# Latent attention and routed FFN layer on eight cores: the key-path evacuation changes engine and the routing of four tiles is batched

## What is computed

```python
x = x + _layernorm(attn(_layernorm(x)))
x = x + _layernorm(ffn(_layernorm(x)))

# attn: latent projections, 32 heads, head dim 128 + 64 rotary
q_c = rmsnorm(h @ w_qa, g_qa)            # 4096 -> 1536
kv  = h @ w_kva                          # 4096 -> 512 + 64
k_c, k_rope = kv[..., :512], kv[..., 512:]
k_c = rmsnorm(k_c, g_kva)                # then w_kvb -> keys, values
# ffn
probs = softmax(xf @ W_router.T)         # 8 experts
topk_p, topk_i = top_k(probs, 2); topk_p /= sum(topk_p)
combine = sum(one_hot(topk_i, 8) * topk_p[..., None], 1)
h = einsum('nd,erd->ner', xf, A_stack) * combine[..., None]
out = xf @ W_base.T + b_base + einsum('ner,eor->no', h, B_stack) * 2.0
```

## Time and profile before

| | |
|---|---|
| times of three runs | 4605.1, 4820.23, 4815.49 us, median 4815.49 us |
| the profiled execution | 4605.1 us |
| its span on the slowest core (core 5) | 4603.5 us |
| spans of the eight cores | 4563.3 to 4603.5 us |
| TensorE busy | 3413.5 us, 74% of the span |
| ScalarE busy | 1351.0 us, 29% |
| VectorE busy | 893.3 us, 19% |

### The profile page before, as it was taken

One profiled execution on the slowest core, in us unless ns is written; L12 is line 12 of the kernel. 1 busy time (PEld: TensorE's weight loads), 2 busy tenths in 40 slices (PEclk: granted clock), 3 DMA queues, 4 the chain that ended last, 5 costly groups with the idle time before them and its releaser, 6 DMA issues. The chain is left out here.

```text
span 4603.5 us, 43117 instructions; the slowest of 8 cores (4563.3 to 4603.5 us)
## 1 busy us (share of the span) xinstructions
PE 3413.5 (74%) x16282; PEld 1345.7 (29%) x16282; DVE 893.3 (19%) x2270; ACT 1351.0 (29%) x2038; POOL 66.6 (1%) x129
## 2 busy tenths in 40 slices
PE   2665683888888898888988889869999048834883
PEld 1333441232232322322222222224444023312331
DVE  3553014111111101111011110100000330023002
ACT  1333001344444444444444434420000230013001
POOL 0000000000000000000000000000000000000000
PEclk9777896898898888988888889879999569966996
DMA  5221411000000000000000000023332326541663
GB/s 132 89 92 45 75 28 30 16 16 3 13 16 15 16 16 1 16 15 16 15 0 16 15 16 1 0 55 73 74 64 46 136 48 110 110 114 33 110 111 109
DMA packets 31370, 218.96 MB, mean 48 GB/s; under 512 B 3888, under 2 KB 4160, under 8 KB 14784
## 3 DMA queue, kind: packets, MB, share of 16 engines
q0 software_dynamic: 17776, 147.97, 17.8%
q1 hardware_dynamic: 13392, 68.24, 4.3%
HBM read 347.37 MB, written 16.78 MB: 79 GB/s over the span
## 5 line engine op out<-in xcount | busy, mean ns | idle before, releaser
L69 ACT ACTIVATE pool<-sPP,pool 128x512 bf16<-128x512 f32 x1024 | 700.2, 687 | 588.7 <-PE sPP L69 588.3
L69 PE MATMUL sPP<-pool 128*128 128x512 bf16 (+1 forms) x2048 | 801.2, 426 | 1.7 <-DVE pool L69 1.7
L69 PE MATMUL PEp<-pool 128*128 128x128 bf16 (+2 forms) x3872 | 534.4, 290 | 171.5 <-DVE pool L69 93.7
L69 PE MATMUL PDq<-pool 128*1 128x512 bf16 (+3 forms) x1792 | 499.0, 338 | 170.7 <-DVE pool L69 125.8
L69 PE MATMUL fP<-pool 128*128 128x512 bf16 (+1 forms) x2176 | 522.6, 398 | 75.3 <-DMA pool<-wbt 37.9
L69 PE MATMUL oP<-pool 128*128 128x512 bf16 x2048 | 457.8, 388 | 57.0 <-ACT pool L69 31.1
L69 DVE BATCH_NORM_STATS2 pool<-pool 128x6 f32<-128x512 bf16 (+1 forms) x344 | 209.6, 679 | 1352.2 <-ACT pool L69 1223.9
L69 PE MATMUL PCq<-pool 128*128 128x512 bf16 x1024 | 430.9, 421 | 0.0
L69 PEld LDWEIGHTS PEp<-pool 128*128 128x128 bf16 (+1 forms) x3872 | 286.3, 97 | 413.0 <-issue 229.1
L69 ACT ACT_TABLE_LOAD x77 | 98.8, 1283 | 882.3 <-PE sPP L69 277.2
L69 DVE COPY pool<-PDq 1x1024 f32<-1x1024 f32 x64 | 78.0, 1218 | 1429.8 <-PEq L1249 1395.2
(11 more groups left out here) (58 smaller groups left out, 1067.3 us busy)
## 6 DMA issues: line engine op xcount, KB each, us to landing
pool<-wbt POOLq DMA_DIRECT2D x64, 1024.0 KB, 8.7
pool<-xb SPq DMA_DIRECT2D x24, 2048.0 KB, 9.3
pool<-wo POOLq DMA_DIRECT2D x16, 2048.0 KB, 12.5
pool<-wqb POOLq DMA_DIRECT2D x16, 1152.0 KB, 10.0
out<-pool SPq DMA_DIRECT2D x64, 256.0 KB, 2.1
pool<-wqa POOLq DMA_DIRECT2D x4, 3072.0 KB, 22.8
pool<-wkvb POOLq DMA_DIRECT2D x16, 512.0 KB, 12.0
pool<-wkva POOLq DMA_DIRECT2D x1, 4608.0 KB, 33.0
```

The costliest lines, as they stand in the source:

```text
L69: r = a(*args, **kw)
```

## The change

Three edits.

1. **Stage A1, the kcT evacuation moves from ScalarE to VectorE.** Its five instructions leave the ScalarE loop and become a section behind `kvchain(it-2)` on VectorE: four `tensor_scalar` (multiply by g_kva) and one `tensor_copy`, behind a wait for the five transposes. The ScalarE loop has 16 iterations instead of 18.
2. **Stage A1, the second inverse square root shares a buffer.** `kvchain` now uses `v_rsqrt`, whose result goes to `col_a[par]` instead of `col_c[par]`. So it may start only when ScalarE has read `col_a[par]` for the tile two further on: a wait for `lnapply(i+2)` is added there, and the wait for `lnapply(i-2)` in `a1_ln` goes.
3. **Stage D.** The statistics chain uses the shared two-buffer helpers (`ln_stats`, `v_rsqrt`, `ln_finish`), with a wait for the apply of the tile two before; it has one instruction less after the root, and no memset. The routing chain is done once for the four tiles of a group: four copies out of `lgP`, then each step on 4 or 32 columns, or four times in a row without waits between where the scalar differs by tile; ScalarE's part is five activations in a row.

```diff
@@ a1_ln
                 S_.wait(v, tok[("ln1s", i)])
-                S_.wait(v, tok.get(("lnapply", i - 2)))
                 v_rsqrt(v, par, mv[par][:, 1:2], LN_EPS)
@@ a1_kvchain
                 S_.wait(v, tok[("kv_ms", i)])
-                v_rsqrtN(v, col_c[par][:], col_c[par][:], rs_x[par][:],
-                         rs_t[par][:], magic_i[:], 1e-30)
+                if i + 2 < KT:
+                    S_.wait(v, tok[("lnapply", i + 2)])
+                v_rsqrt(v, par, col_c[par][:], 1e-30)
                 tok[("kv_sq", i)] = sigV.inc(v.last)
...
+            @blk.vector
+            def _(v):
+                v = LastW(v)
+                S_.wait(v, tok[("kcT_mm", i)])
+                for k in range(KVK):
+                    v.tensor_scalar(out=k_cT[:, k, i * 128:(i + 1) * 128],
+                                    in0=trP[par][:, k * 128:(k + 1) * 128],
+                                    scalar1=gkva_b[:, k:k + 1], scalar2=None,
+                                    op0=ALU.mult)
+                v.tensor_copy(out=k_ropeT[:, i * 128:(i + 1) * 128],
+                              in_=trP[par][0:RD, KVK * 128:KVK * 128 + 128])
+                tok[("kcT_evac", i)] = sigV.inc(v.last)
@@ the ScalarE loop of A1
-                if i >= 2:
-                    ik = i - 2
-                    pk = ik % 2
-                    S_.wait(s, tok[("kcT_mm", ik)])
-                    for k in range(KVK):
-                        s.activation(out=k_cT[:, k, ik * 128:(ik + 1) * 128],
...
-                    s.copy(out=k_ropeT[:, ik * 128:(ik + 1) * 128],
-                           in_=trP[pk][0:RD, KVK * 128:KVK * 128 + 128])
@@ stage D, the routing
-                    S_.wait(v, tok.get(("tk_exp", ti - 1)))
-                    v.tensor_copy(out=lg_sb[:], in_=lgP[:])
...
+                for tg in range(GT):
+                    ti = grp * GT + tg
                     S_.wait(v, tok[("lg_mm", ti)])
+                    v.tensor_copy(out=lgB[:, tg, :], in_=lgP[:])
+                    tok[("lg_used", ti)] = sigV.inc(v.last)
+                S_.wait(v, tok[("lg_used", grp * GT + GT - 1)])
+                v.reduce_max(out=m1B[:], in_=lgB[:], axis=AX.X)
...
+                tok[("tk1", grp)] = sigV.inc(v.last)
+                S_.wait(v, tok[("tk_exp", grp)])
```

More of the change, by code:

```diff
@@ L536, in _ @@
                 S_.wait(v, t)
-                v.reciprocal(out=col_c[par][:], in_=col_c[par][:])
+                v.reciprocal(out=col_a[par][:], in_=col_a[par][:])
                 t = sigV.inc(v.last)
@@ L606, in _ @@
             s = LastW(s)
-            for i in range(KT + 2):
+            for i in range(KT):
                 par = i % 2
-                if i >= 2:
-                    ik = i - 2
-                    pk = ik % 2
-                    S_.wait(s, tok[("kcT_mm", ik)])
-                    for k in range(KVK):
-                        s.activation(out=k_cT[:, k, ik * 128:(ik + 1) * 128],
-                                     in_=trP[pk][:, k * 128:(k + 1) * 128],
-                                     func=AF.Identity,
-                                     scale=gkva_b[:, k:k + 1], bias=0.0)
-                    s.copy(out=k_ropeT[:, ik * 128:(ik + 1) * 128],
-                           in_=trP[pk][0:RD, KVK * 128:KVK * 128 + 128])
-                    tk = sigS.inc(s.last)
[L621 to L640, removed]
@@ new lines, in _ @@
+                S_.wait(s, tok[("ln1fin", i)])
+                S_.wait(s, tok[("xload", i)])
+                S_.wait(s, tok.get(("lnT_mm_all", i - 2)))
+                s.activation(out=ln1_bufs[par][:], in_=x_bufs[par][:],
+                             func=AF.Identity,
+                             scale=col_a[par][:], bias=col_b[par][:])
+                tk = sigS.inc(s.last)
+                assert tk == tok[("lnapply", i)]
+                for wv in range(nwA):
+                    S_.wait(s, tok[("lnT_mm", i, wv)])
+                    nk = min(16, DK - wv * 16)
+                    if i < QT:
+                        dst = ln1T_own[:, i, wv * 16 * 128:(wv * 16 + nk) * 128]
+                    else:
+                        dst = ln1T_tmps[par][:, wv * 16 * 128:(wv * 16 + nk) * 128]
+                    s.copy(out=dst, in_=trP[par][:, 0:nk * 128])
+                    tk = sigS.inc(s.last)
+                    assert tk == tok[("lnT_evac", i, wv)]
@@ L1610, in build_program @@
                 tok[("ln2T_done", ti)] = tok[("ln2T_ev", ti, nw - 1)]
[L1611 to L1613 removed]
+            tok[("tk_exp", grp)] = (sigS, pS0 + off + GT * (nw + 1) + 1)
             pT0 = sigT.count
@@ L1651, in _ @@
[L1651 to L1660, removed]
@@ new lines, in _ @@
+                S_.wait(v, tok[("lg_used", grp * GT + GT - 1)])
+                v.reduce_max(out=m1B[:], in_=lgB[:], axis=AX.X)
+                t = sigV.inc(v.last)
+                S_.wait(v, t)
+                for tg in range(GT):
+                    v.tensor_scalar(out=mskB[:, tg, :], in0=lgB[:, tg, :],
+                                    scalar1=m1B[:, tg:tg + 1],
+                                    scalar2=None, op0=ALU.is_equal)
+                t = sigV.inc(v.last)
+                S_.wait(v, t)
@@ new lines, in _ @@
+                v.scalar_tensor_tensor(out=mskB[:], in0=mskB[:],
+                                       scalar=-1e30, in1=lgB[:],
+                                       op0=ALU.mult, op1=ALU.add)
+                t = sigV.inc(v.last)
+                S_.wait(v, t)
+                v.reduce_max(out=m2B[:], in_=mskB[:], axis=AX.X)
+                t = sigV.inc(v.last)
+                S_.wait(v, t)
+                v.tensor_scalar(out=rcolA[:], in0=m1B[:], scalar1=-1.0,
+                                scalar2=None, op0=ALU.mult)
@@ new lines, in _ @@
+                t = sigV.inc(v.last)
+                S_.wait(v, t)
+                for tg in range(GT):
+                    v.tensor_scalar(out=mskB[:, tg, :], in0=lgB[:, tg, :],
+                                    scalar1=m2B[:, tg:tg + 1],
+                                    scalar2=None, op0=ALU.is_ge)
+                t = sigV.inc(v.last)
+                S_.wait(v, t)
+                v.tensor_tensor(out=explB[:], in0=explB[:], in1=mskB[:],
+                                op=ALU.mult)
@@ L1687, in _ @@
+                t = sigV.inc(v.last)
+                S_.wait(v, t)
+                for tg in range(GT):
+                    ti = grp * GT + tg
+                    v.tensor_scalar(out=comb_g[:, tg, :], in0=explB[:, tg, :],
+                                    scalar1=colcB[:, tg:tg + 1], scalar2=2.0,
                                     op0=ALU.mult, op1=ALU.mult)
```

143 lines of the change are left out of this document (45 added, 98 removed).

## The result

The changed kernel took 0.9904 of the time of the kernel before (95% interval 0.9886 to 0.9923), about 44 us less (36 to 53 us of some 4604). Its profiled execution took 4558.33 us. Of twelve executions each, the medians are 4621.72 and 4659.78 us; about half of the executions of either kernel have one or both dies at a lower granted clock, which lifts both medians, and the ratio above leaves these out. It was forecast 35 us faster, 0.8%; the gain is there, at 1.0% somewhat larger, and within the 2% as said.

The account below looks back on a forecast made before the run. The prediction took a chain of handovers, in A1 ScalarE and TensorE in series, to bound the kernel. From 4605.1 us it took 25.7 for stage A1 and 9.5 for stage D, giving 4570 us (4550 to 4602).

Parts of the forecast that it names:

- What bounds A1 before: Stage A1: ScalarE and TensorE in series, the apply behind the kcT evacuation; period 23.90 us, VectorE not in the loop.
- A serial loop through VectorE comes next: Stage A1 after the change: VectorE's queue, with apply and evacuation as links, sets a 22.2 us period; A1 gives 25.7 us.
- the five handovers: Stage A1's new loop: releases between engines, 0.5 to 0.9 us a period in all, taken as 0.7.
- What the evacuation costs on VectorE: Stage A1: five kcT evacuations behind a kv chain, not in the trace there; 0.20 us each taken, 0.70 the far end.
- the near bound: Stage A1: each kcT evacuation on VectorE takes 0.20 us, so five take 1.00.
- The rival of a dear evacuation: Stage A1: evacuations at 0.70 us each, period 24.7, total 4607 us; chance 0.11, shared with a VectorE loop well over 22.4.
- The clock rivals: TensorE in A1: kv matmuls all at 1.2 GHz, 4614 us, chance 0.06; or kept at 2.4 GHz, 4567 us, chance 0.10.
- Stage D: Routing once per group saves 4.5 us a group, statistics chain 0.27 us; two groups 9.5 us, between 6 and 12.
- The load of the query weights passes the gain on: After A1: TensorE idles 44.48 us for this load, so A1's saving counts in full; the rival, hidden anyway, chance 0.03.
- The sum: Whole kernel: 25.7 us from stage A1 and 9.5 us from stage D come off 4605.1 us.
- The absolute time: Whole kernel: 4570 us, with 4550 to 4602 as the range, some 0.85 likely.
- I do not forecast against it: Base of the forecast: the 4815.49 us median, from two executions some 4.6% longer, set aside for the profiled 4605.1 us.

Follow-up runs that it names:

- e5: Kernel before the change with a fourth Newton step in stage A1's norm chain on VectorE; stage A1 took 398.2 us, against 396.2 without the step.
- e6: Changed kernel with the kcT evacuation on ScalarE, behind the apply two tiles further on, and the kv root in its own column; A1 took 329.5 us.
- e4: Changed kernel with a fourth Newton step in stage A1's norm chain on VectorE; stage A1 took 383.5 us, against 367.1 without the step.
- e3: Changed kernel with the kv root in its own column again, evacuation still on VectorE; stage A1 took 338.3 us, against 367.1.
- e8: As e6, but with the kcT transposes in the other parity's trP; A1 took 305.8 us, whole time 0.9792 of the kernel before.

## Why the prediction was right or wrong

- **What bounds A1 before**: right. The same microsecond on VectorE costs nothing there once the loop runs (e5), and taking the evacuation from ahead of the apply, with nothing else, takes 66.7 us off (e6).
- **A serial loop through VectorE comes next**: right in every link and shown by e4 and e3. Its size was taken at 22.2 us and is 21.94. The terms that were mis-sized: the five handovers, taken as 0.7, measured 0.51 (0.15, 0.11, 0.14, 0.11 and nothing ahead of the next statistics, which start while the last evacuation ends), and the evacuations, taken as 1.00, measured 0.91. On core 5 the last evacuation ends at 423.3 and not at 426.9. The twelve periods, 263.3 us instead of 266.4, make 3.1 us of that; the loop starts 0.3 later than forecast; behind the apply of tile 15 another 0.9 is gained, and that is the clock and not the handovers: the first wave of transposes of that tile takes 1.05 us, and the prediction had taken it as before, 1.86. So A1 gave 29.1 us and not 25.7. Some tiles have a small instruction that starts late on VectorE (0.30 us of idle time ahead of it in the iteration shown, 0.1 in others), which is now on the path: so the periods lie between 21.79 and 22.15.
- **What the evacuation costs on VectorE**: the near bound held, 0.86 for four blocks. The rival of a dear evacuation is out. (Its limit of 1.7 us a period was that of A1 alone, 25.7 over fifteen; the whole kernel would have turned slower from 2.3 on, 35.2 over fifteen.) The Trainium skill's rule (VectorE: DVE Perf Modes, Specifications) that ScalarE sits closer to PSUM does not decide here: from the five transposes to the next ones it is 1.24 us with VectorE (changed kernel, e3) and 1.51 with ScalarE (e6).
- **The clock rivals**: the clock got slightly better, though not where the prediction looked. The kv matmuls hardly changed: 9.28 us in the iteration shown is the shortest on core 5, and the median of all tiles and cores is 10.15 against 10.35 before. The first wave of transposes did, 1.46 us in the mean against 1.86. As the prediction said of that case, it could not show while VectorE's loop set the pace, but for the last tile. In e6 and in the early periods of e8, where TensorE sets it, it did. The rule that the prediction quotes there (the Trainium skill, TensorE: Matmul & The Clock Gate, Loop structure matters more than you think) is of a copy behind which the next matmuls follow immediately; here TensorE stands waiting for the copy or the apply, so the trace of before does not speak against it.
- **Stage D**: right, 9.5 us forecast, 4.6 and 4.9 measured.
- **The load of the query weights passes the gain on**: right.
- **The sum**: 35.2 us forecast, 40.1 by the stages (29.1, 9.5, and 1.5 in the query stage, which the change does not touch), 44 (36 to 53) by the ratio. The 1.5 us are not explained, but they have an order: the stage takes 260.8 to 261.7 in the five kernels whose key path is evacuated on VectorE and 261.9 to 262.4 in the seven that evacuate it on ScalarE. The ratio is of the slowest cores. The median span of all cores, over the executions that the ratio takes, is 4544.6 us for the changed kernel, and 4585.2 to 4587.9 for the kernel before in the three later comparisons: 41 to 43 us, close to the sum of the stages.
- **The absolute time**: 4570 us (4550 to 4602) was made against the one execution whose profile was shown. The profiled execution, 4558.33, lies inside; the median of all twelve, 4621.72, lies outside. The step that failed is "I do not forecast against it": the prediction saw two of three executions 4.6% longer and put their part in the time at nothing, without a reason. In its place the twelve executions of the kernel before show a median of 4659.78 us, 54.7 above the 4605.1 that the sum starts from, and those of the changed kernel one 51.8 above the forecast. The difference of the medians is 38 us, near the 35.2 forecast: the sum had the gain right and its base wrong. The median that was shown would not have helped, since 4815.49 less 35.2 is 4780. Why executions differ so, no run of this case shows.
- **What I did not see**: that the new wait for the apply, which the prediction counted as a link of 3.8 us less 1.67, was optional (e3). The prediction priced the loop but not its alternatives.

## What to carry to other kernels

When an in-order queue ties a ready job to a late one, emitting the late one behind it removes the tie, while moving it to another engine moves the tie there. In A1, with nothing else changed, the first took 66.7 us off (e6, for no added instruction) and the second 57.9 (e3). A scratch column or a PSUM buffer shared by two chains is a wait as well, 2.2 us a tile for the column (e3) and 1.7 for the buffer once nothing else was slower (e8). And a microsecond of harmless work on one engine, in both kernels, tells who sets the pace: it costs its full price or nothing.

## What was not expected of the hardware

- TensorE's own work got shorter when a wait ahead of it went. In the kernel before, the first wave of 16 transposes takes 1.86 us behind an idle time of 5.22; its granted clock is 0.50 of full speed, 1.2 GHz. Below are the wave and its row by stretch, columns as in the earlier trace rows:

```profile
328.18 1.86 PE L69 MATMUL trP<-pool 128*128 128x128 bf16 x16 [5.22 <-ACT pool L69]
...
328.18:330.04 1.86, 1.86 (x16) 1.59 (x16) 1.13 (x7) 0.00 (x0) 0.00 (x0) 0.50 0.00 0
```

  In e6 the same wave takes 1.05 us at a granted clock of 1.00, 2.4 GHz:

```profile
276.44:277.49 1.05, 1.05 (x16) 0.88 (x16) 0.63 (x5) 0.00 (x0) 0.00 (x0) 1.00 0.00 0
```

  Over the 112 first waves of all cores that follow five kcT transposes in the same buffer:

| run | TensorE idle ahead of the five (median, us) | idle ahead of the wave (median, us) | first wave (mean, us) |
|---|---|---|---|
| before | 0 | 5.22 | 1.86 |
| e4 | 3.33 | 1.24 | 1.72 |
| after | 2.34 | 1.24 | 1.46 |
| e3 | 0.60 | 1.24 | 1.15 |
| e6 | 0 | 1.51 | 1.05 |

  e4 gives TensorE the same instructions as the changed kernel and differs only in how long TensorE waits for VectorE, and its waves are longer. In e6 this makes 0.8 us a period, some 10 of the 13 us by which it came out below its expectation. In e8 both waves gain at first; its twelve periods make 13 of the 21 us, and where the rest lies can't be read from the expectation, which does not show its head and tail.
- VectorE starts the next statistics 0.07 us before its last evacuation has ended in the records (284.36 against 284.23 + 0.20); independent instructions on it overlap, and four of 8 columns take 0.63 us where dependent ones stand 0.27 apart.
